# Loading a chunk's edge attributes in five pieces, each begun when the gathers of the preceding piece have landed

## The chip, the cores and the metric

The kernel runs on one core of a Trainium2 chip. The metric is the device time of one execution in microseconds (us), lower is better; of the kernel before it is the median of two runs without the profiler.

## What is computed

A graph has 12,500 nodes with 64 features and 400,000 edges, sorted by destination node. Each edge carries the features of its source node, multiplied by one 64 x 64 matrix, plus its own 64 attributes, multiplied by another, all times a weight. The edges' messages are summed at their destination nodes, added to the nodes, and each node is normalized.

```python
h = feat_src @ node_w.T
rf = review_feat @ review_w.T
m = (h[src_idx] + rf) * edge_w
agg = jax.ops.segment_sum(m, dst_idx, num_segments=12500)
x = _layernorm(x + agg, axis=-1)
```

## The kernel before

Since the matrices can be applied after the sum, the kernel sums 128 raw values per edge (64 features of the source node, 64 attributes) into `sums` at the destination nodes, and multiplies at the end. It does so for two kinds of edges in two ways.

**Gathered edges.** The first 88 chunks of 3200 edges. A chunk lies in one of four slots (`SLOTS`) of `rows`, as 25 tiles of 128 edges (`TILES`, one edge per partition and tile), 64 gathered features and 64 attributes side by side. POOL (`gather_chunk`, L366) fetches the features with one indirect DMA per tile, 25 per chunk. The 25 tiles form five parts of five (`PARTS`, `PER_PART`), and `gathered[s][q]` counts the landings of part q in slot s. Before the first gather of a chunk POOL waits until the chunk's list of source nodes has landed (`src_landed`) and the slot is free (`slot_free`). SP (`load_chunk`) waits for `slot_free` and then loads the chunk's `src`, `dst`, weights and attributes (L310, L313 to L315), the attributes in one DMA of 800 KB. DVE (`add_chunk`) makes a 128 x 128 matrix per tile that says which edge goes to which of 128 nodes, with its weight (`scatter`, L441, three buffers of one part each). PE (`sum_chunk`, L839) multiplies 25 of those by the tiles of `rows` into `window_ps`; it waits for `gathered` and `scatter_ready` before each part. DVE adds the window to `sums` (L453) and then sets `slot_free`.

**Counted edges.** The other 118,400 edges, in 52 groups of 18 tiles (the first has 7). PE and DVE count for each how often a source node occurs (L881, with DVE's L495 and L497; ACT copies each count out, L744), and PE multiplies the counts by the table of nodes held on the chip (`sum_x`, L896, twice 49 pairs per group). ACT loads a group's attributes (`g_attr`, L716, 576 KB) after it has read the counts of the group before.

**Order.** Each engine's program is written out by hand. A step of PE is: sum a chunk, count the 18 tiles of a group, sum a second chunk in three steps of five, then `sum_x`. Eight chunks and five groups make a round (`STEPS` = 2, 1, 2, 1, 2). POOL does nothing but gathers until the last chunk and scales eight blocks of the output afterwards. SP's queue is in order: the four slots are filled first, then 84 chunks as slots come free, then the stores of the output (L351), which wait for ACT and POOL to scale the blocks. After chunk 85 DVE and PE finish all blocks of nodes that chunks 86 and 87 don't reach (`early`), then sum those two chunks and finish the `late` blocks.

Of the kernel before, what the change touches and what calls it, by code (L numbers as in the profile page):

```python
# [36 lines left out]
TILES = 25  # L37
SLOTS = 4
PARTS = 5
# [13 lines left out]
def build(nc, x, src, dst, attr, weight, node_w, review_w, out):  # L53
    NODES, F = x.shape
    EDGES = src.shape[0]
    CHUNK = P * TILES
# [6 lines left out]
    PER_PART = TILES // PARTS  # L63
# [34 lines left out]
    with ExitStack() as ctx:  # L98
        def sb(name, shape, dt=F32):
            return ctx.enter_context(nc.sbuf_tensor(name, shape, dt))  # L100
# [4 lines left out]
        def sem(name):  # L105
            return ctx.enter_context(nc.semaphore(name))
# [4 lines left out]
        rows = sb("rows", [P, SLOTS, TILES, 2 * F])  # L111
# [99 lines left out]
        w_t_ready = sem("w_t_ready")  # L211
        src_landed = [sem(f"src_landed{s}") for s in range(SLOTS)]
        edge_landed = [sem(f"edge_landed{s}") for s in range(SLOTS)]
        gathers_begun = sem("gathers_begun")
        gathered = [[sem(f"gathered{s}_{q}") for q in range(PARTS)] for s in range(SLOTS)]
        slot_free = [sem(f"slot_free{s}") for s in range(SLOTS)]
# [40 lines left out]
        def by_partition(dram, c):  # L257

            return dram[bass.ds(c * CHUNK, CHUNK)].rearrange("(p k) -> p k", k=TILES)
# [36 lines left out]
        def each_chunk(eng, first, until, do):  # L296

            rounds = range(-(-first // SLOTS), until // SLOTS)
            for c in range(first, rounds[0] * SLOTS):
                do(*at_slot(c))  # L300
            with eng.Fori(rounds[0], rounds[-1] + 1) as r:
                for s in range(SLOTS):
                    do(r * SLOTS + s, s, r)
            for c in range((rounds[-1] + 1) * SLOTS, until):
                do(*at_slot(c))

        @block.sync
        def _(sp):
            def load_src(c, s):
                sp.dma_start(src_sb[s][:, :], by_partition(src, c)).then_inc(src_landed[s], 16)  # L310

            def load_rest(c, s):
                sp.dma_start(dst_sb[s][:, :], by_partition(dst, c)).then_inc(edge_landed[s], 16)  # L313
                sp.dma_start(w_sb[s][:, :], by_partition(weights, c)).then_inc(edge_landed[s], 16)
                sp.dma_start(rows[:, s, :, F:2 * F],  # L315
                             attr[bass.ds(c * CHUNK, CHUNK), :].rearrange("(p k) f -> p k f", k=TILES)
                             ).then_inc(edge_landed[s], 16)

            def load_chunk(c, s, r):

                sp.wait_ge(slot_free[s], r + 1)
                load_src(c, s)
                load_rest(c, s)

            for s in range(SLOTS):
                load_src(s, s)
            sp.dma_start(dst_i[:, 0, :], dst.rearrange("(c e) -> c e", e=CHUNK)).then_inc(dst_loaded, 16)

            sp.dma_start(g_dst[1:GROUPS, :, :], dst[COUNTED_FROM + GT0 * P:EDGES].rearrange(
                "(g t e) -> g t e", t=GT, e=P)).then_inc(g_dst_loaded, 16)  # L330
            for t0 in range(0, GT, GT0):
                n = min(GT0, GT - t0)
                sp.dma_start(g_dst[0:1, t0:t0 + n, :], dst[COUNTED_FROM:COUNTED_FROM + n * P].rearrange(
                    "(a t e) -> a t e", a=1, e=P)).then_inc(g_dst_loaded, 16)
            sp.dma_start(w_both[:, 0:F], node_w).then_inc(w_loaded, 16)
            sp.dma_start(w_both[:, F:2 * F], review_w).then_inc(w_loaded, 16)
            for s in range(SLOTS):
                load_rest(s, s)
            each_chunk(sp, SLOTS, CHUNKS, load_chunk)

            sp.wait_ge(tables_ready, 1)
            with sp.If(is_narrow(sp) == 0):
                each_chunk(sp, CHUNKS, ALL_CHUNKS, load_chunk)
            for n, b in enumerate(early + late):
                h0, j = blocks[b]
                if n < ACT_BLOCKS:
                    sp.wait_ge(act_scaled, n + 1)
                else:
                    sp.wait_ge(pool_scaled, n - ACT_BLOCKS + 1)
                whole = min(j, BY_P - h0)  # L350
                sp.dma_start(out[h0 * P:(h0 + whole) * P, :].rearrange("(h l) f -> l h f", l=P),  # L351
                             x_tab[:, h0:h0 + whole, :]).then_inc(stored, 16)
                if whole < j:
                    sp.dma_start(out[BY_P * P:NODES, :], x_tab[0:NODES - BY_P * P, BY_P, :]).then_inc(stored, 16)
            sp.wait_ge(stored, 16 * (BLOCKS + (BY_P < HI)))
# [53 lines left out]
        def _(dve):  # L409
# [9 lines left out]
            def add_chunk(c, s, r, first=None):  # L419


                base = dve.value_load(base_tab[0:1, bass.ds(c, 1)], min_val=0, max_val=NODES - 1)  # L422
                if first is None:
                    first = dve.value_load(window_tab[0:1, bass.ds(c, 1)], min_val=0, max_val=ALL_WINDOWS)
                until = dve.value_load(window_tab[0:1, bass.ds(c + 1, 1)], min_val=0, max_val=ALL_WINDOWS)  # L425

                dve.wait_ge(edge_landed[s], (r + 1) * 48)

                dve.wait_ge(left_ready, first + c + 1)
                dve.tensor_scalar(dst_left[:, :], dst_sb[s][:, :], lo_all[:, bass.ds(c, 1)], None, ALU.subtract  # L430
                                  ).then_inc(left_ready, 1)
                with dve.Fori(first, until) as w:

                    dve.wait_ge(left_ready, w + c + 2)
                    for q in range(PARTS):

                        if q >= PART_BUFS:
                            dve.wait_ge(part_used[q - PART_BUFS], w + 1)
                        for i in range(PER_PART):
                            k = q * PER_PART + i  # L440
                            made = dve.tensor_scalar(scatter[:, q % PART_BUFS, i, :], column[:, :],  # L441
                                                     dst_left[:, k:k + 1], w_sb[s][:, k:k + 1],
                                                     ALU.is_equal, ALU.mult)
                        made.then_inc(scatter_ready[q], 1)

                    dve.wait_ge(window_summed, w + 1)
                    dve.wait_ge(window_added, w + 1)
                    dve.tensor_scalar(dst_left[:, :], dst_left[:, :], float(WIN), None, ALU.subtract  # L448
                                      ).then_inc(left_ready, 1)
                    to = nc.s_assert_within(  # L450
                        base + (w - first) * WIN, 0, NODES - 1, skip_runtime_bounds_check_because=
                        "a chunk's last window begins at or before its largest dst, which is a node")
                    dve.tensor_tensor(sums[:, bass.ds(to, WIN)], sums[:, bass.ds(to, WIN)],  # L453
                                      window_ps[:, 0:WIN], ALU.add).then_inc(window_added, 1)

                dve.sem_inc(slot_free[s], 1)
                return until
# [364 lines left out]
        def _(pe):  # L822
            def sum_chunk(c, s, r, first=None):

                if first is None:
                    first = pe.value_load(window_tab[0:1, bass.ds(c, 1)], min_val=0, max_val=ALL_WINDOWS)
                until = pe.value_load(window_tab[0:1, bass.ds(c + 1, 1)], min_val=0, max_val=ALL_WINDOWS)
                with pe.Fori(first, until) as w:

                    pe.wait_ge(edge_landed[s], (r + 1) * 48)  # L830

                    pe.wait_ge(window_added, w + 1)
                    for k in range(TILES):
                        if k % PER_PART == 0:
                            pe.wait_ge(scatter_ready[k // PER_PART], w + 1)

                            pe.wait_ge(gathered[s][k // PER_PART], (r + 1) * (16 * PER_PART))
                        q, i = divmod(k, PER_PART)
                        done = pe.matmul(window_ps[:, 0:WIN], rows[:, s, k, :], scatter[:, q % PART_BUFS, i, :],  # L839
                                         start=(k == 0), stop=(k == TILES - 1))  # L840
                        if i == PER_PART - 1 and q < PARTS - PART_BUFS:
                            done.then_inc(part_used[q], 1)
                    done.then_inc(window_summed, 1)
                return until
# [157 lines left out]
```

## Time and profile before

| | us |
|---|---|
| median of 2 runs without the profiler | 2815.59 (2814.23 to 2816.95) |
| span of the profiled execution | 4978.1 |
| PE busy in it | 2706.6 |
| POOL busy in it | 2097.5 |
| DVE busy in it | 1848.4 |
| ACT busy in it | 832.4 |

The profiled execution took much longer than those that are timed, so shares of its span are not shares of the time. Durations of single instructions, gaps between instructions that wait for nothing, and the times from an issue to what it releases are what is to be read from it. SPq and ACTq are the queues of SP and ACT, whose DMA issues are not counted as busy; PEclk is the granted TensorE clock as a share of full speed.

### The profile page before, as it was taken

How to read it: one execution, taken by the hardware profiler on the slowest of the kernel's cores; microseconds unless marked ns; L12 is line 12 of the kernel's file. 1: busy time of each engine (PE TensorE's matmuls, PEld its weight loads, DVE VectorE, ACT ScalarE, POOL GpSimd, SP SyncE). 2: the span in 40 equal slices, each digit the busy share in tenths (PEclk: the TensorE clock that was granted, in tenths of full speed). 3: DMA queues.
4: the chain of work that ended last, by engine and by line, in shares of the span. 5: the costliest groups of instructions: out<-in, count | busy, mean ns of one | idle time of the engine just before them, and what ended most of it. 6: DMA issues, size and time to landing. Idle time of an engine off the chain costs nothing.

```text
span 4978.1 us, 63532 instructions
## 1 busy us (share of the span) xinstructions
PE 2706.6 (54%) x22003; PEld 2036.4 (41%) x22004; DVE 1848.4 (37%) x7016; ACT 832.4 (17%) x1327; POOL 2097.5 (42%) x2223
## 2 busy tenths in 40 slices
PE   0555555545655545555456555555554556455465
PEld 0343444434443434444344434344443444344345
DVE  3333333423442333333334424333333344333344
ACT  0111111111121111121111211111111112111112
POOL 7343343443334443444433344434444333544432
PEclk9776777767776767777667767677776777667677
DMA  4111121111111111211111211112111112112111
GB/s 98 37 34 37 34 42 38 34 36 38 37 38 38 34 35 38 41 38 34 35 38 35 42 37 35 34 38 42 38 34 35 37 36 42 37 34 43 36 35 38
DMA packets 531458, 192.11 MB, mean 39 GB/s; under 512 B 489893, under 2 KB 495772, under 8 KB 530975
## 3 DMA queue, kind: packets, MB, share of 16 engines
q1 hardware_dynamic: 334128, 80.80, 8.6%
q0 software_dynamic: 70400, 72.23, 6.6%
q10 hardware_dynamic: 126623, 34.94, 3.2%
q8 instruction: 198, 3.24, 0.3%
q14 instruction: 109, 0.89, 0.1%
HBM read 184.60 MB, written 3.20 MB: 38 GB/s over the span
## 4 chain that ended last, share of the span: by engine, by line
PE 43%; another core or an unknown queue 28%; issue 21%; DVE 4%; ACT 2%; DVEq 1%; ACTq 1%; POOLq 0%; POOL 0%
PE x_sums_ps L896 15%; PE count_ps L881 15%; PE window_ps L839 11%; ACT counts L744 2%; DVE scatter L441 1%; DVE hot_lo L497 1%; PE attr_ps L873 1%; ACTq L771 0%; PE turn_ps L858 0%; PE turn_ps L855 0%; DVEq L422 0%; DVEq L425 0%; DVE hot_key L495 0%; PE count_ps L924 0%
## 5 line engine op out<-in xcount | busy, mean ns | idle before, releaser
L366 POOL DMA_INDIRECT rows<-x,src x2200 | 2088.8, 949 | 2791.5 <-DMA src<-src 2146.3
L881 PE MATMUL count_ps<-hot_key,hot_lo 128*128 128x343 bf16 x5550 | 1157.4, 361 | 1294.2 <-ACT counts L744 839.0
L896 PE MATMUL x_sums_ps<-counts,x_tab 128*64 128x126 f32 (+1 forms) x10192 | 865.5, 302 | 790.2 <-issue 775.0
L881 PEld LDWEIGHTS count_ps<-hot_key,hot_lo 128*128 128x128 bf16 x5550 | 570.1, 113 | 1726.5 <-issue 1092.5
L896 PEld LDWEIGHTS x_sums_ps<-counts,x_tab 128*64 128x64 f32 x10192 | 692.5, 154 | 948.4 <-issue 927.3
L744 ACT ACTIVATE counts<-count_ps 128x686 f32<-128x686 f32 x925 | 737.3, 802 | 1784.9 <-remote 1335.6
L495 DVE TENSOR_SCALAR hot_key<-count,cols 128x686 bf16<-128x686 f16 x925 | 377.8, 408 | 1550.8 <-remote 1272.3
L441 DVE TENSOR_SCALAR scatter<-column,dst_left,w 128x128 f32<-128x128 f32 x2200 | 588.3, 347 | 576.2 <-PE window_ps L839 503.0
L497 DVE TENSOR_SCALAR hot_lo<-count,cols 128x128 bf16<-128x128 f16 x2775 | 721.7, 323 | 4.9 <-issue 4.9
L839 PE MATMUL window_ps<-scatter,rows 128*128 128x128 f32 x4400 | 563.1, 289 | 85.2 <-issue 55.4
L839 PEld LDWEIGHTS window_ps<-scatter,rows 128*128 128x128 f32 x4400 | 535.0, 200 | 120.9 <-issue 108.8
L510 DVE TENSOR_TENSOR hot_rel<-column,cols 128x126 f32<-128x126 f32 (+1 forms) x52 | 15.2, 292 | 645.1 <-issue 441.8
L873 PEld LDWEIGHTS attr_ps<-hot_rel,g_attr 128*128 128x128 f32 x926 | 189.0, 228 | 45.1 <-issue 9.5
L726 ACT ACTIVATE slot_rel<-turn_ps,slot_no 126x1 f32<-126x1 f32 (+1 forms) x52 | 13.6, 262 | 979.2 <-remote 625.3
L873 PE MATMUL attr_ps<-hot_rel,g_attr 128*128 128x14 f32 x926 | 155.2, 243 | 12.6 <-remote 12.6
L759 ACT ACTIVATE x_sums<-x_sums_ps 128x126 f32<-128x126 f32 (+1 forms) x52 | 14.3, 276 | 881.9 <-PE x_sums_ps L896 881.9
L734 ACT ACTIVATE slot_rows<-x_sums_ps 126x128 f32<-126x128 f32 x52 | 14.4, 278 | 400.8 <-PE x_sums_ps L905 400.8
L448 DVE TENSOR_SCALAR dst_left<-dst_left 128x25 f32<-128x25 f32 x88 | 15.8, 180 | 146.8 <-PE window_ps L839 146.8
L531 DVE TENSOR_TENSOR sums<-sums,turn_ps 128x128 f32 x52 | 15.0, 289 | 76.2 <-PE turn_ps L911 43.0
L430 DVE TENSOR_SCALAR dst_left<-dst,lo_all 128x25 f32<-128x25 int32 x88 | 22.3, 254 | 50.2 <-issue 50.2
L405 POOL TENSOR_TENSOR x_tab<-x_tab,counts 128x512 f32<-128x512 f32 (+2 forms) x8 | 5.9, 748 | 79.7 <-DVE counts L573 79.6
L855 PE MATMUL turn_ps<-tile_first,spread 18*126 18x1 f32 (+1 forms) x104 | 19.4, 253 | 33.7 <-DVE packed L484 33.7
(112 smaller groups left out, 557.5 us busy)
## 6 DMA issues: line engine op xcount, KB each, us to landing
rows<-edge_attr SPq DMA_DIRECT2D x88, 800.0 KB
rows<-x,src POOLq DMA_INDIRECT x2200
g_attr<-edge_attr ACTq DMA_DIRECT2D x51, 576.0 KB
out<-x_tab SPq DMA_DIRECT2D x11, 256.0 KB
counts<-dst SPq DMA_DIRECT2D x1, 1562.5 KB
src<-src SPq DMA_DIRECT2D x88, 12.5 KB, 1.7
dst<-dst SPq DMA_DIRECT2D x88, 12.5 KB
w<-edge_weight SPq DMA_DIRECT2D x88, 12.5 KB
```

The costliest lines, as they stand in the source:

```text
L366: pool.indirect_dma_start(out=rows[:, s, k, 0:F], out_offset=None, in_=x, in_offset=bass.IndirectOffsetOnAxis(ap=src_sb[s][:, k:k + 1].bit ...
L430: dve.tensor_scalar(dst_left[:, :], dst_sb[s][:, :], lo_all[:, bass.ds(c, 1)], None, ALU.subtract).then_inc(left_ready, 1)
L441: made = dve.tensor_scalar(scatter[:, q % PART_BUFS, i, :], column[:, :], dst_left[:, k:k + 1], w_sb[s][:, k:k + 1], ALU.is_equal, ALU.mult)
L448: dve.tensor_scalar(dst_left[:, :], dst_left[:, :], float(WIN), None, ALU.subtract).then_inc(left_ready, 1)
L495: dve.tensor_scalar(hot_key[h][:, :], count16[:, :], cols[:, KEY, t:t + 1], None, ALU.is_equal)
L497: made = dve.tensor_scalar(hot_lo[h][:, i, :], count16[:, 0:P], cols[:, LO, t:t + 1], cols[:, part, t:t + 1], ALU.is_equal, ALU.mult)
L744: act.activation(counts[:, :, t * SPAN:(t + 1) * SPAN].rearrange("p (a h) d -> p a h d", a=2), count_ps[t % 2][:, :, 0:HALF].rearrange("p ...
L839: done = pe.matmul(window_ps[:, 0:WIN], rows[:, s, k, :], scatter[:, q % PART_BUFS, i, :], start=(k == 0), stop=(k == TILES - 1))
L855: pe.matmul(turn_ps[0:nt * SPAN, REL_COL:REL_COL + 1], spread[0:nt, 0:nt * SPAN], tile_first[0:nt, 0:1], start=True, stop=True)
L873: pe.matmul(attr_ps[0:(until - t) * F, t * SPAN:until * SPAN], g_attr[:, t:until, :].rearrange("p t f -> p (t f)"), hot_rel[:, t:until, :] ...
L881: last = pe.matmul(count_ps[b][:, a, 0:HALF], hot_lo[h][:, i, :], hot_key[h][:, a * HALF:(a + 1) * HALF], start=(i == 0), stop=(i == 2))
L896: done = pe.matmul(x_sums_ps[half * F:(half + 1) * F, 0:ns], x_tab[:, hi, :], counts[:, hi, 0:ns], start=(hi < 2), stop=(hi >= HI - 2))
```

## The change

The one DMA that loads a chunk's attributes becomes five, one for each part of five tiles (128 x 5 x 64 values, 160 KB). They have semaphores of their own, `attr_landed`, one per slot. For the first four chunks the five are issued in a row. For each of the 84 chunks after them SP issues the first at once, and before piece q waits until part q-1 of the gathers of the same chunk has landed. DVE's wait for `dst` and the weights falls from 48 to 32, since two DMAs are left on `edge_landed`, and PE waits before a window for these and for all five pieces.

```diff
--- before.py
+++ after.py
@@ -211,6 +211,7 @@
         w_t_ready = sem("w_t_ready")
         src_landed = [sem(f"src_landed{s}") for s in range(SLOTS)]
         edge_landed = [sem(f"edge_landed{s}") for s in range(SLOTS)]
+        attr_landed = [sem(f"attr_landed{s}") for s in range(SLOTS)]
         gathers_begun = sem("gathers_begun")
         gathered = [[sem(f"gathered{s}_{q}") for q in range(PARTS)] for s in range(SLOTS)]
         slot_free = [sem(f"slot_free{s}") for s in range(SLOTS)]
@@ -309,18 +310,30 @@
             def load_src(c, s):
                 sp.dma_start(src_sb[s][:, :], by_partition(src, c)).then_inc(src_landed[s], 16)
 
-            def load_rest(c, s):
+            def load_edges(c, s):
                 sp.dma_start(dst_sb[s][:, :], by_partition(dst, c)).then_inc(edge_landed[s], 16)
                 sp.dma_start(w_sb[s][:, :], by_partition(weights, c)).then_inc(edge_landed[s], 16)
-                sp.dma_start(rows[:, s, :, F:2 * F],
-                             attr[bass.ds(c * CHUNK, CHUNK), :].rearrange("(p k) f -> p k f", k=TILES)
-                             ).then_inc(edge_landed[s], 16)
+
+            def load_attr_part(c, s, q):
+                ks = slice(q * PER_PART, (q + 1) * PER_PART)
+                sp.dma_start(rows[:, s, ks, F:2 * F],
+                             attr[bass.ds(c * CHUNK, CHUNK), :].rearrange("(p k) f -> p k f", k=TILES)[:, ks, :]
+                             ).then_inc(attr_landed[s], 16)
+
+            def load_rest(c, s):
+                load_edges(c, s)
+                for q in range(PARTS):
+                    load_attr_part(c, s, q)
 
             def load_chunk(c, s, r):
 
                 sp.wait_ge(slot_free[s], r + 1)
                 load_src(c, s)
-                load_rest(c, s)
+                load_edges(c, s)
+                load_attr_part(c, s, 0)
+                for q in range(1, PARTS):
+                    sp.wait_ge(gathered[s][q - 1], (r + 1) * (16 * PER_PART))
+                    load_attr_part(c, s, q)
 
             for s in range(SLOTS):
                 load_src(s, s)
@@ -424,7 +437,7 @@
                     first = dve.value_load(window_tab[0:1, bass.ds(c, 1)], min_val=0, max_val=ALL_WINDOWS)
                 until = dve.value_load(window_tab[0:1, bass.ds(c + 1, 1)], min_val=0, max_val=ALL_WINDOWS)
 
-                dve.wait_ge(edge_landed[s], (r + 1) * 48)
+                dve.wait_ge(edge_landed[s], (r + 1) * 32)
 
                 dve.wait_ge(left_ready, first + c + 1)
                 dve.tensor_scalar(dst_left[:, :], dst_sb[s][:, :], lo_all[:, bass.ds(c, 1)], None, ALU.subtract
@@ -827,7 +840,8 @@
                 until = pe.value_load(window_tab[0:1, bass.ds(c + 1, 1)], min_val=0, max_val=ALL_WINDOWS)
                 with pe.Fori(first, until) as w:
 
-                    pe.wait_ge(edge_landed[s], (r + 1) * 48)
+                    pe.wait_ge(edge_landed[s], (r + 1) * 32)
+                    pe.wait_ge(attr_landed[s], (r + 1) * (16 * PARTS))
 
                     pe.wait_ge(window_added, w + 1)
                     for k in range(TILES):
```

SP's queue, in the loop over the rounds of four slots. What stood there for slots 1 and 2 (a row "ISA" is a wait or an address):

```order
L310 ISA [waits slot_free1]
L310 DMA src<-src 128x25
L313 DMA dst<-dst 128x25
L314 DMA w<-edge_weight 128x25
L315 ISA
L315 DMA rows<-edge_attr 128x25x64
L310 ISA [waits slot_free2]
L310 DMA src<-src 128x25
```

And what stands there now, from the first attribute piece of slot 1 to the first load of slot 2 (the three small loads of slot 1 stand ahead of it as before):

```order
L319 DMA rows<-edge_attr 128x5x64
L319 ISA [waits gathered1_0]
L319 DMA rows<-edge_attr 128x5x64
L319 ISA [waits gathered1_1]
L319 DMA rows<-edge_attr 128x5x64
L319 ISA [waits gathered1_2]
L319 DMA rows<-edge_attr 128x5x64
L319 ISA [waits gathered1_3]
L319 DMA rows<-edge_attr 128x5x64
L311 ISA [waits slot_free2]
L311 DMA src<-src 128x25
```

The loads of slot 2 now stand behind four waits for the gathers of slot 1.

PE's queue, at the first window of a chunk in slot 0. Before:

```order
L832 REGISTER_ALU [waits edge_landed0]
L837 REGISTER_ALU [waits scatter_ready0,window_added]
L839 MATMUL window_ps<-scatter,rows 128x128 [waits gathered0_0]
L839 MATMUL window_ps<-scatter,rows 128x128 x4
L839 MATMUL window_ps<-scatter,rows 128x128 [waits gathered0_1,scatter_ready1]
```

Now:

```order
L844 REGISTER_ALU [waits edge_landed0]
L846 REGISTER_ALU [waits attr_landed0]
L853 MATMUL window_ps<-scatter,rows 128x128 [waits gathered0_0,scatter_ready0,window_added]
L853 MATMUL window_ps<-scatter,rows 128x128 x4
L853 MATMUL window_ps<-scatter,rows 128x128 [waits gathered0_1,scatter_ready1]
```

The wait for all five pieces stands ahead of the first matmul of the window; the waits for single parts of the gathers are where they were.

## Rows read from the trace of the kernel before

**Rows 1.** the page: span, and busy time of each engine (share of the span), x instructions.

```profile
span 4978.1 us, 63532 instructions
...
PE 2706.6 (54%) x22003; PEld 2036.4 (41%) x22004; DVE 1848.4 (37%) x7016; ACT 832.4 (17%) x1327; POOL 2097.5 (42%) x2223
```

**Rows 2.** the waits: engine, line, waited for: us in total, times, longest.

```profile
POOL rows L366 <- DMA src<-src: 2146.3, 84, 40.2
ACT counts L744 <- remote: 1335.6, 186, 20.2
...
POOL rows L366 <- issue: 645.2, 2116, 0.7
```

**Rows 3.** the waits of SP's queue, same columns.

```profile
SPq L310 <- DVEq L456: 4596.1, 84, 104.8
```

**Rows 4.** groups by line: count, busy us, mean ns, idle before and its releaser.

```profile
L366 POOL DMA_INDIRECT rows<-x,src x2200 | 2088.8, 949 | 2791.5 <-DMA src<-src 2146.3
```

**Rows 5.** timeline of POOL: start us, us, engine, line, operation, count, idle before.

```profile
4.43 1.12 POOL L366 DMA_INDIRECT rows<-x,src  x1 [0.66 <-issue]
...
34.56 0.95 POOL L366 DMA_INDIRECT rows<-x,src  x1 [0.30 <-issue]
35.81 0.94 POOL L366 DMA_INDIRECT rows<-x,src  x1 [0.30 <-issue]
...
4883.11 0.94 POOL L366 DMA_INDIRECT rows<-x,src  x1 [0.30 <-issue]
```

**Rows 6.** timeline of PE, same columns; then windows with the granted clock (PEclk).

```profile
2048.46 6.32 PE L839 MATMUL window_ps<-scatter,rows 128*128 128x128 f32 x50 [0.53 <-DVE scatter L441]
...
2054.94 5.59 PE L896 MATMUL x_sums_ps<-counts,x_tab 128*64 128x126 f32 x98
...
2150.51 2.02 PE L881 MATMUL count_ps<-hot_key,hot_lo 128*128 128x343 bf16 x12
...
core 0: us, PE busy (x) PEld busy (x) DVE busy (x) ACT busy (x) POOL busy (x), PEclk, DMA share, GB/s
2048.50:2054.70 6.20, 6.20 (x51) 5.94 (x52) 4.85 (x19) 0.58 (x3) 0.00 (x0) 1.00 0.46 98
2055.00:2060.40 5.40, 5.40 (x99) 5.29 (x98) 2.76 (x13) 0.00 (x0) 1.96 (x2) 1.00 0.49 100
```

**Rows 7.** timeline of all engines around two chunk loads, same columns.

```profile
2001.71 0.29 DVE L453 TENSOR_TENSOR sums<-sums,window_ps 128x128 f32 x1
...
2002.11 0.34 SPq L310 DMA_DIRECT2D src<-src  x1
...
2003.59 0.56 SPq L315 DMA_DIRECT2D rows<-edge_attr  x1
...
2004.64 0.94 POOL L366 DMA_INDIRECT rows<-x,src  x1 [25.95 <-DMA src<-src]
...
2034.75 0.94 POOL L366 DMA_INDIRECT rows<-x,src  x1 [0.31 <-issue]
...
2055.49 0.34 SPq L310 DMA_DIRECT2D src<-src  x1
...
2058.02 1.02 POOL L366 DMA_INDIRECT rows<-x,src  x1 [22.33 <-DMA src<-src]
```

**Rows 8.** DMA in 2035.6 to 2036.3, 2036.3 to 2036.9, 2036.9 to 2048.9: packets, MB, rate or share.

```profile
DMA packets 0, 0.00 MB, mean 0 GB/s; under 512 B 0, under 2 KB 0, under 8 KB 0
...
q0 software_dynamic: 32, 0.03, 28.3%
...
DMA packets 1, 0.02 MB, mean 1 GB/s; under 512 B 0, under 2 KB 0, under 8 KB 0
```

**Rows 9.** DMA queues in 2004.6 to 2008.2 (three rows), then in 2004.9 to 2009.5.

```profile
DMA packets 2949, 0.76 MB, mean 212 GB/s; under 512 B 2948, under 2 KB 2948, under 8 KB 2948
...
q1 hardware_dynamic: 2948, 0.75, 104.6%
q14 instruction: 1, 0.01, 1.2%
...
q1 hardware_dynamic: 3216, 0.82, 90.6%
q0 software_dynamic: 89, 0.09, 8.8%
```

**Rows 10.** the ACT issue of g_attr, and the DMA queues in 2048.9 to 2052.4.

```profile
2048.13 0.40 ACTq L716 DMA_DIRECT2D g_attr<-edge_attr  x1
...
q10 hardware_dynamic: 2320, 0.59, 80.8%
```

**Rows 11.** timeline of the end, all engines.

```profile
4942.41 17.16 SPq L351 DMA_DIRECT2D out<-x_tab  x13
...
4955.03 7.18 PE L839 MATMUL window_ps<-scatter,rows 128*128 128x128 f32 x50 [3.68 <-issue]
4959.61 1.07 SPq L354 DMA_DIRECT2D out<-x_tab  x1
```

## Prediction

> **What bounds the kernel now.** I first read the span on the page: the profiled execution took 4978.1 us [rows 1], against a median of 2815.6 us for the runs without the profiler. So the profile is 1.77 times as long as what is to be predicted, and the first question is where its extra 2162 us lie. The list of waits answers: POOL, which issues the 2200 gathers, idled 2146.3 us in 84 pieces before the first gather of a chunk, waiting for its `src` load [rows 2]. That load is not slow. SP's own waits show why it is late: SP sat 4596.1 us, also 84 times, for DVE's `slot_free` [rows 3]. The slots came free late, because in the profiled execution PE, DVE and ACT stood still for long stretches: the copy of the counts alone waited 1335.6 us for something that the profile doesn't name, up to 20 us at a time [rows 2].
>
> The groups by line then give POOL's own pace: a gather is busy for 949 ns [rows 4] and 645.2 us of issue gaps lie over 2116 of them [rows 2], 0.305 us each. One gather takes 1.254 us, a chunk of 25 takes 31.4 us, and all take 2088.8 + 645.2 = 2734 us. They start at 4.4 us [rows 5]. 2815.6 - 4.4 - 2734 leaves 77 us for everything behind the last gather and for all stalls; in the profile the time behind the start of the last gather at 4883.1 is 95 us [rows 5]. So without the profiler POOL hardly waits, and it is the bound. The chunk boundary at 35.81 us, where everything was loaded ahead, shows that a chunk then begins with the ordinary gap of 0.30 us [rows 5].
>
> PE is second. Where the granted clock is 1.00, the upper of its two levels, a window of 25 tiles takes 6.3 us, half a sum over x 5.6 us and two counted tiles 2.0 us [rows 6]. A step with its 18 tiles and 1.6 chunks is about 18.2 + 11.2 + 10.1 = 39.5 us, against 1.6 x 31.4 = 50 us of POOL. So PE catches up with the gathers and then waits for them, while POOL stays three chunks (94 us) ahead of the slot that it needs next. Before the change SP has that lead too: it loads a chunk as soon as its slot is free.
>
> **The change, part by part.** *Same bytes.* 800 KB per chunk and 3200 pieces of 256 bytes go as before; four more issues and four waits per chunk cost nothing on SP, which idles [rows 3]. DVE needs only the two small loads (its wait falls from 48 to 32) and was never short of the third: 0. At the start (four slots filled with no wait) nothing but the number of issues changes.
>
> *SP loses its lead.* This is what matters. SP now stands in the middle of chunk n, waiting for its gathers, and behind that wait are queued the loads of chunk n+1, `src` first. POOL cannot begin n+1 without them. So each of the 84 chunks after the first four gets a chain that must fit into the time of its last five gathers. From the start of chunk n, in us:
> - tile 19, the last of the fourth part, starts at 19 x 1.254 = 23.8;
> - it lands at most 2.15 later, at 26.0: a gather issued at 2034.75 [rows 7] had no packet before 2036.3, its 32 packets until 2036.9 and none after [rows 8];
> - SP wakes 0.1 later, as it does when DVE frees a slot (2001.71 + 0.29 to 2002.11) [rows 7]: 26.1;
> - it issues the fifth piece, at most the 0.56 of the whole load [rows 7] and a gap of 0.1: 26.8;
> - from the issue of `src` to the first gather is 2.53 us, at 2002.11 to 2004.64 and at 2055.49 to 2058.02 [rows 7]: 29.3;
> - the `src` packets queue behind those of the piece in the same ring. The burst of the whole load, 3216 packets, took 4.6 us [rows 9], so 640 packets take 0.9. The delay is 0 to 0.9; I take all: 30.2.
>
> POOL needs it at 31.4. The slack is 1.2 us (2.1 with no queueing), so the undisturbed chain is hidden and POOL's pace stays.
>
> *Disturbed chains.* ACT loads 576 KB of `g_attr` for each group, a burst of 2320 packets from 2048.9 to at most 2052.4 after an issue at 2048.13 [rows 10]. What a burst does to a gather is seen at 2004.64: it had no packet of its own until 2008.2 [rows 9], 3.6 us after its issue where 1.55 is usual [rows 8], so 2.0 us late. When does the `g_attr` burst fall? PE ends a window some 3.8 us into the next chunk's gathers (below), counts 18 tiles in 18.2, and ACT issues at 22.0; packets run from 22.8 to 26.3. The gather of tile 19 has its packets at 25.4 to 26.0, inside that. This holds for the three steps of five whose first chunk finds PE waiting, 31 of the 51 loads. In the other two PE comes some 5 us later out of a sum over x, and the burst meets the `src` load or nothing. A chain late by 2.0 stalls POOL for 2.0 - 1.2 = 0.8 us, or for nothing with the slack of 2.1. I take the middle, 0.4 us, x 31 = 12 us. Bounds: 0, and 0.8 x 51 = 41 us.
>
> *PE waits for all five pieces.* It used to start a window when the first gathers were there; now it starts when the fifth piece has landed, at 26.1 + 1.4 + 0.9 = 28.4 (the whole load had its first packets 1.3 to 1.4 us after its issue [rows 7, 9]). A window is 6.3 to 7.2 us [rows 6, 11], so it ends at 34.7 to 35.6. Before, it ended a fifth of a window behind the last landing, 30.1 + 2.15 + 1.3 = 33.6. For all chunks but the last these 1 to 2 us are covered by POOL's lead of 94 us; the last one sets the end: +2 us.
>
> *The stores.* SP cannot store the early blocks until it has issued the fifth piece of chunk 87. The thirteen stores took 17.2 us of issue in the profile and ended at 4959.6, before the last window did at 4962.2 [rows 11]. They start here some 10 us later than before and still end before the late blocks are ready: 0, at most 5 us.
>
> **Sum.** 0 + 12 + 2 = 14 us. The terms are durations of gathers, packets and issues, which I take over unscaled to the unprofiled 2815.6: 2830 us. For the profiled execution itself the sum is different: its slots come free 50 us apart and more (SP's `src` issues at 2002.11 and 2055.49 [rows 7]), longer than the 29 us for which SP is tied up, so the chain costs nothing there and the span should be 4978 + 2 = 4980, within 1%. The profile will hide the stall that I expect without the profiler.
>
> **Rivals.**
> 1. *The bursts cost nothing*: the slack is nearer 2.1, or the `g_attr` loads fall elsewhere, or PE is the bound without the profiler after all (2706.6 us busy at a mixed clock [rows 1]), so that slots come free late as in the profile. For it: the queueing term was taken at its bound. Against it: the 3.6 us of that one gather. Time: 2815.6 + 2 = 2818. The Trainium skill says the same by another way: "DMA: Bandwidth & Descriptors", section "Queues, rings and completion order", has each DMA engine round-robin between queues and change after some 9 to 17 descriptors, so a gather would never wait for a whole burst. By the packet pace of this trace, 4.6 us for 200 packets on an engine [rows 9], 17 of them are 0.4 us, less than the slack, which gives 2818. The gather at 2004.64 speaks against that rule, since no packet of it moved for 3.6 us.
> 2. *Slower: the chain is too long in every chunk.* Place: POOL before the first gather of each of 84 chunks, waiting for `src`. It decides (2%, 56 us, is 0.67 us per chunk) from a chain 1.9 us longer than my sum. For it: six terms in a row, none ever seen in this combination; a gather delayed by 2.0 in each chunk would give 0.8 x 84 = 67 us, and `src` delayed by another 2.0 gives 2.8 x 84 = 235 us. Against it: four of the six terms stand in rows, and the rest is taken at its bound. Time, midway: 2815.6 + 150 = 2966.
> 3. *A little faster*: the burst of 3200 packets at a chunk's load no longer disturbs the gathers. Gathers average 949 ns where the undisturbed ones are 0.94 us [rows 4, 5]: at most some 9 ns x 2200 = 20 us, of which half may belong to DVE or `g_attr`. Time: 2806. Landings of gathers are not on POOL's path, so nothing more can come.
>
> **How the numbers follow.** The forecast of 2830: 0.38. Nothing but the tail, 2818: 0.30. Too long in every chunk, 2966: 0.17. A little faster: 0.07. The remaining 0.08 are stalls of 45 to 80 us from more collisions than counted. Within 2% is 2759 to 2872, about what a measurement of this kernel can tell from no change. It takes in the forecast, rivals 1 and 3 and most of the rest: 0.80. Slower is 0.18, faster 0.02, since no term exceeds 20 us of gain. The range of 2806 to 2885 leaves out most of rival 2 and little else.
>
> **What would show it.** In the profile after: five attr issues per chunk, four of them 6.3 us apart; SP waiting for gathers; POOL's first gather of a chunk never more than 2.6 us behind its `src` issue; POOL's total wait for `src` near 2146. POOL's gathers should stay at 949 ns. If the median is above 2872, the chain is longer than 33 us and the term at fault is the landing or the `src` load behind the piece. If it is 2818 or less, bursts don't delay gathers enough. If the span of the profile grows by over 1%, then SP's order bites even where slots come free 50 us apart.

## The result and the profile after

The changed kernel takes 2850.09 us (2843.94 and 2856.24), the kernel before 2815.59: 1.0126 times as long, 95% interval 1.0071 to 1.0181 (two runs of each), so 20 to 51 us slower. The forecast was 2830 in a range of 2806 to 2885.

One thing must be said ahead of all rows. These kernels have two paces, far apart: the kernel before takes 2812 to 2817 us on some chips and 4916 to 5006 on others. The two times above are of the first kind, and so is the profile of the changed kernel. The profile of before (4978.1 us, [rows 1]) was of the second. I call them quick and slow chips.

Page of the changed kernel, on a quick chip: span, busy times, the chain that ended last, POOL's group (count, busy us, mean ns, idle before).

```profile
span 2854.4 us, 64593 instructions
...
PE 2231.2 (78%) x22003; PEld 1851.0 (65%) x22004; DVE 1813.1 (64%) x7016; ACT 838.0 (29%) x1327; POOL 2128.2 (75%) x2223
...
POOL 67%; issue 24%; DMA 7%; SPq 1%; PE 0%; DVE 0%; POOLq 0%; ACT 0%; DVEq 0%
...
L379 POOL DMA_INDIRECT rows<-x,src x2200 | 2119.6, 963 | 704.9 <-issue 661.7
```

Its waits (engine, line, waited for: us in total, times, longest), and then those of SP's queue.

```profile
POOL rows L379 <- issue: 661.7, 2170, 0.7
...
PE window_ps L853 <- DMA rows<-edge_attr: 499.7, 51, 24.1
...
POOL rows L379 <- DMA src<-src: 43.2, 30, 3.0
```

```profile
SPq L319 <- DMA rows<-x,src: 2361.8, 334, 56.2
SPq L311 <- DVEq L469: 20.5, 1, 20.5
```

Beside [rows 2 to 4]: POOL's wait for `src` is 43.2 us in 30 pieces instead of 2146.3 in 84. SP no longer waits for a free slot (one time, at the start) but for gathers, 334 of the 336 times. POOL is the bound: 2119.6 + 661.7 + 43.2 = 2824.5 us from the first gather at 4.4, and 26 us of finish. Without waits the same sum has 30 more ordinary gaps of 0.305 in place of the 43.2: the pure stall is 43.2 - 9.2 = 34.0 us, where 34.5 (20 to 51) were lost. One of the 30 is no longer than an ordinary gap, so there are 29 stalls. PE's 499.7 us of waiting for the pieces hold nobody up before the last chunk, since no slot is waited for after the start.

**One stall.** The chain that ended last shows what the stalls are made of (start, us, what), in two places.

```profile
1344.97 4.72 DMA rows<-x,src
...
1350.41 2.14 DMA src<-src
...
1409.11 4.12 DMA rows<-x,src
1414.37 2.02 DMA src<-src
```

The gather that begins at 1344.97 is tile 19 of its chunk. It lands 4.72 us later. The one that begins at 1377.15, in the next chunk, is tile 19 with nothing in its way. The timelines of ACT, SP and POOL around both (start, us, engine, line; POOL's idle time before in brackets):

```profile
1344.93 0.40 ACTq L729 DMA_DIRECT2D g_attr<-edge_attr  x1
...
1350.41 0.37 SPq L311 DMA_DIRECT2D src<-src  x1
...
1353.38 0.94 POOL L379 DMA_INDIRECT rows<-x,src  x1 [1.20 <-DMA src<-src]
...
1377.15 0.95 POOL L379 DMA_INDIRECT rows<-x,src  x1 [0.31 <-issue]
...
1380.26 0.39 SPq L311 DMA_DIRECT2D src<-src  x1
...
1384.64 0.95 POOL L379 DMA_INDIRECT rows<-x,src  x1 [0.30 <-issue]
```

In the free chunk `src` is issued 3.11 us after tile 19 began. In the other ACT issued `g_attr` in the same moment as tile 19; `src` was issued after 5.44 us, 2.33 later, and the first gather of the next chunk came 8.41 us after tile 19 instead of 7.49. From the issue of `src` to that gather are 2.97 us. So the free chain is 3.11 + 2.97 = 6.08 us, the slack 1.41, and 2.33 - 1.41 = 0.92 is the stall (1.20 less the ordinary 0.30).

**Longer stalls.** Here the burst comes later, at the `src` load itself:

```profile
316.40 0.40 ACTq L729 DMA_DIRECT2D g_attr<-edge_attr  x1
...
317.33 0.38 SPq L311 DMA_DIRECT2D src<-src  x1
...
323.79 0.95 POOL L379 DMA_INDIRECT rows<-x,src  x1 [2.37 <-DMA src<-src]
```

`src` was issued in time, and the gather came 6.46 us after it instead of 2.97: 3.49 us late, the length of a whole `g_attr` burst (3.5 us at most, [rows 10]).

The longest wait of all is again one of tile 19, which begins at 1922.44 (the chain, then the timeline):

```profile
1922.44 6.03 DMA rows<-x,src
```

```profile
1922.12 0.40 ACTq L729 DMA_DIRECT2D g_attr<-edge_attr  x1
...
1929.62 0.34 SPq L311 DMA_DIRECT2D src<-src  x1
...
1932.67 0.94 POOL L379 DMA_INDIRECT rows<-x,src  x1 [3.04 <-DMA src<-src]
```

Of the 16 parts in which this gather's landing is counted, 15 were there after 4.45 us, as in the first stall, and the last after 6.03. A last part more than 1 us behind the others is found in the three longest waits (3.04, 2.97 and 2.60 us) and in no other. In each of the three, one 16 KB packet of the instruction queue began 3.2 to 3.8 us after tile 19 and took 1.2 to 1.3 us; such packets stand beside several shorter stalls too, and no run tests whether it is what held up the last part.

**All stalls.** ACT's issues of `g_attr` from the fifth chunk on, by their distance from the start of tile 19 of the chunk in which they fall:

| issued | loads | followed by a stall |
|---|---|---|
| 19.1 to 6.3 us before tile 19 | 3 | 0 |
| 0.4 before to 2.3 after | 29 | 29 |
| 3.6 to 6.6 after | 17 | 0 |

No chunk without such a load has a stall. In 22 of the 29 the landing of tile 19 is late, so that `src` is issued 4.4 to 7.3 us after it (3.1 to 3.9 in chunks with no load of `g_attr`). In the other 7 `src` goes out in time and its own load is late. This ties the loss of POOL to the bursts in the complete kernel, at the quick pace, by the trace alone.

### The profile page after: what moved, and what is told of

The parts are those of the page before. It is cut to its first block, busy times and chain, and to the rows that moved or that the text cites. A ratio compares the mean times of both kernels' runs of the same rounds, so it can differ in the third digit from the quotient of the medians.

```text
span 2854.4 us, 64593 instructions
## 1 busy us (share of the span) xinstructions
PE 2231.2 (78%) x22003; PEld 1851.0 (65%) x22004; DVE 1813.1 (64%) x7016; ACT 838.0 (29%) x1327; POOL 2128.2 (75%) x2223
## 4 chain that ended last, share of the span: by engine, by line
POOL 67%; issue 24%; DMA 7%; SPq 1%; PE 0%; DVE 0%; POOLq 0%; ACT 0%; DVEq 0%
POOL rows L379 67%; DMA rows<-x,src 4%; DMA src<-src 3%; SPq L319 0%; PE window_ps L853 0%; DVE scatter L454 0%; SPq L311 0%; DMA rows<-edge_attr 0%; POOLq L302 0%; POOLq L377 0%; SPq L302 0%; POOL count L387 0%; DVE x_tab L562 0%; DVE counts L581 0%; POOLq L98 0%
## 5 line engine op out<-in xcount | busy, mean ns | idle before, releaser
L379 POOL DMA_INDIRECT rows<-x,src x2200 | 2119.6, 963 | 704.9 <-issue 661.7
L853 PE MATMUL window_ps<-scatter,rows 128*128 128x128 f32 x4400 | 631.1, 310 | 543.7 <-DMA rows<-edge_attr 499.7
L853 PEld LDWEIGHTS window_ps<-scatter,rows 128*128 128x128 f32 x4400 | 604.7, 222 | 577.9 <-issue 560.9
L895 PE MATMUL count_ps<-hot_key,hot_lo 128*128 128x343 bf16 x5550 | 933.5, 310 | 0.0
L895 PEld LDWEIGHTS count_ps<-hot_key,hot_lo 128*128 128x128 bf16 x5550 | 507.8, 102 | 304.9 <-issue 116.4
L910 PE MATMUL x_sums_ps<-counts,x_tab 128*64 128x126 f32 (+1 forms) x10192 | 576.1, 271 | 13.1 <-ACT counts L757 13.0
L910 PEld LDWEIGHTS x_sums_ps<-counts,x_tab 128*64 128x64 f32 x10192 | 551.7, 137 | 22.4 <-ACT counts L757 15.4
L887 PEld LDWEIGHTS attr_ps<-hot_rel,g_attr 128*128 128x128 f32 x926 | 154.5, 190 | 27.3 <-issue 7.3
L887 PE MATMUL attr_ps<-hot_rel,g_attr 128*128 128x14 f32 x926 | 136.5, 222 | 7.0 <-DVE hot_lo L510 7.0
L466 DVE TENSOR_TENSOR sums<-sums,window_ps 128x128 f32 x88 | 25.4, 288 | 5.3
## 6 DMA issues: line engine op xcount, KB each, us to landing
src<-src SPq DMA_DIRECT2D x88, 12.5 KB
dst<-dst SPq DMA_DIRECT2D x88, 12.5 KB
w<-edge_weight SPq DMA_DIRECT2D x88, 12.5 KB
```

The costliest lines, as they stand in the source:

```text
L379: pool.indirect_dma_start(out=rows[:, s, k, 0:F], out_offset=None, in_=x, in_offset=bass.IndirectOffsetOnAxis(ap=src_sb[s][:, k:k + 1].bit ...
L887: pe.matmul(attr_ps[0:(until - t) * F, t * SPAN:until * SPAN], g_attr[:, t:until, :].rearrange("p t f -> p (t f)"), hot_rel[:, t:until, :] ...
L895: last = pe.matmul(count_ps[b][:, a, 0:HALF], hot_lo[h][:, i, :], hot_key[h][:, a * HALF:(a + 1) * HALF], start=(i == 0), stop=(i == 2))
L910: done = pe.matmul(x_sums_ps[half * F:(half + 1) * F, 0:ns], x_tab[:, hi, :], counts[:, hi, 0:ns], start=(hi < 2), stop=(hi >= HI - 2))
```

## The experiments

Three theories. **A**: the loss is POOL waiting for `src`, which SP now issues behind its waits for gathers, in chunks where a `g_attr` burst uses up the slack. **B**: the pieces themselves, more DMAs and later ones beside the gathers, slow POOL or the landings. **C**: the chain is too long in every chunk.

### First four, on a slow chip

The changed kernel again:

> The changed kernel once more, on the chip of the next three runs, to measure its loss beside them. Both theories: 1.0126 times the kernel before, within 0.5%. In its profile POOL's first gather of about 30 of the 83 later chunks waits for src, 35 us over the ordinary gaps in all.

Then with `src`, `dst` and weights one chunk ahead:

```diff
     load_attr_part(c, s, 0)
+    load_next_small(c, s, r)      # waits slot_free of the next slot; src, dst, weights of c + 1
     for q in range(1, PARTS):
         sp.wait_ge(gathered[s][q - 1], (r + 1) * (16 * PER_PART))
         load_attr_part(c, s, q)
```

> The changed kernel, but SP issues src, dst and weights of chunk n+1 behind the first attribute piece of chunk n, ahead of the four waits for gathers. Theory A (the loss is POOL waiting for a src load that is queued behind those waits): POOL's stalls for src vanish, 35 us come back, and what is left is the later start of PE's last window: 2815 + 5 = 2820 us, ratio to the kernel before 1.002. Theory B (the pieces themselves, more DMAs beside the gathers, slow POOL or the landings): the time stays at 2850, ratio 1.012.

Without the waits:

```diff
     for q in range(1, PARTS):
-        sp.wait_ge(gathered[s][q - 1], (r + 1) * (16 * PER_PART))
         load_attr_part(c, s, q)
```

> The changed kernel without the waits for gathers: five pieces, issued in a row as soon as the slot is free; PE still waits for all five. Theory A: SP keeps its lead, so no stall for src, and the pieces of the last chunk have landed long before PE needs them: 2815 us, ratio 1.000. Theory B (five DMAs instead of one cost time by their number): 2830 to 2850. The span of its profile is open: near 2820 if the pieces by themselves free the profiled execution of its standstills, near 4980 if their spacing does it.

And with the last wait one part later:

```diff
-        sp.wait_ge(gathered[s][q - 1], (r + 1) * (16 * PER_PART))
+        sp.wait_ge(gathered[s][q if q == PARTS - 1 else q - 1], (r + 1) * (16 * PER_PART))
```

> The changed kernel, but the fifth piece waits for the landing of the fifth part of the gathers instead of the fourth, so that SP is tied up for five gathers (6.3 us) longer. Theory A with the sum of the chain as the profile of the changed kernel shows it (2.6 + 0.6 + 3.0 = 6.2 us from tile 19 to the first gather, against 7.5 available): 1.3 us of slack become a stall of 5.0 us at each of 84 chunks, 2817 + 84 x 5.0 = 3240 us, and some 50 us more from g_attr bursts that no slack absorbs: 3240 to 3300, ratio 1.15 to 1.17. Theory B: 2855, since the number of DMAs is the same.

| kernel | us | ratio to before (4987.15 us), 95% |
|---|---|---|
| changed | 5001.08 | 1.0027 (1.0014 to 1.0039) |
| src ahead | 5015.66 | 1.0057 (1.0037 to 1.0077) |
| no waits | 5019.89 | 1.0066 (1.0046 to 1.0086) |
| last wait a part later | 5014.55 | 1.0056 (1.0037 to 1.0075) |

Hardly any of the expectations could be tested here, since they were written for the other pace; the 1.0126 expected of the changed kernel was missed with 1.0027. Even the kernel whose chain is 6.3 us longer in each chunk, which should have cost over 400 us, lies with the rest. The waits of the changed kernel on this chip say why; POOL's first, then SP's:

```profile
POOL rows L379 <- DMA src<-src: 2176.0, 84, 41.1
ACT counts L757 <- remote: 1236.5, 159, 20.9
```

```profile
SPq L311 <- DVEq L469: 2280.3, 84, 102.6
SPq L319 <- DMA rows<-x,src: 423.5, 73, 8.6
```

They are those of [rows 2, 3]: slots come free late, SP is mostly done with a chunk's pieces before the next slot is free, and its order hardly matters. That is what the prediction said of the profiled execution (it forecast a span within 1% of 4978; it is 5005.5, +0.5%). What it shows for the question is little: all four take 0.3 to 0.7% longer than the kernel before at this pace, the three variants more than the changed kernel and not told apart from each other, and no run separates the number of DMAs from PE's wait for all five. One part of the third expectation falls: the pieces do not end the standstills, with or without their spacing (spans 5005.5 and 5015.7).

The kernel with `src` ahead ran twice more, on two further occasions:

> The changed kernel with src, dst and weights of the next chunk issued ahead of the four waits for gathers, once more, since the first time the kernel before itself took 4987 us. If the kernel before takes about 2815 us here: theory A (the loss is POOL waiting for src behind SP's waits): ratio 1.002, and its profile shows no boundary gap over 0.4 us between chunks; theory B (the pieces slow POOL or the landings): ratio 1.012. If the kernel before takes about 4980 us, both: 1.003 to 1.007, as in the first time, since slots come free too late for SP's order to matter.

> The changed kernel with src, dst and weights of the next chunk issued ahead of the four waits for gathers, on another chip. If the kernel before takes about 2815 us here: theory A (the loss is POOL waiting for src behind SP's waits): ratio 1.002, no gap over 0.4 us between chunks on POOL; theory B (the pieces slow POOL): ratio 1.012. If the kernel before takes about 4985 us: 1.003 to 1.007 as twice already.

Both were slow chips again: 5021.43 against 4994.02 (1.0055, 1.0041 to 1.0069) and 4972.64 against 4920.08 (1.0098, 1.0080 to 1.0116), the second above the 1.007 expected. So this repair of the complete kernel has never been timed at the quick pace.

### A cut-down in which POOL is the bound on any chip

PE does one matmul per window, DVE one scatter matrix, and the counted edges are left out; SP and POOL do for the 88 chunks what they did. In the version with bursts ACT loads 576 KB into `g_attr` for each chunk. The edit, shortened (`...`):

```diff
+    dve.tensor_scalar(scatter[:, 0, 0, :], ...)           # one tile instead of 25
+    pe.matmul(window_ps[:, 0:WIN], rows[:, s, TILES - 1, :], scatter[:, 0, 0, :], start=True, stop=True)
+    # bursts, on ACT, for each chunk from the fifth on:
+    act.wait_ge(gathered[s][3], (r + 1) * (16 * PER_PART))
+    act.dma_start(g_attr[:, :, :], ...)
```

> A cut-down of the kernel before, meant to make POOL the bound whatever the chip: the counted edges are left out on all engines, PE does one matmul per chunk and DVE one scatter matrix, so the output is not the reference's. SP's and POOL's programs are those of the kernel before. If the other engines no longer hold POOL up: 84 x 25 gathers and more at 1.254 us, last gather begun at 4.4 + 2199 x 1.254 = 2762 us, no boundary gap between chunks over 0.4 us, and some 50 us of finish: 2815 us. If it still takes over 4000 us, the standstills do not come from the work of PE, DVE and ACT, and nothing below can be read.

> The same cut-down with SP's program of the changed kernel: five pieces, four waits for gathers, no g_attr loads at all. Theory A (a chain of 6.2 us from tile 19 to the next chunk's first gather, in 7.5 us): every chain fits, boundary gaps stay at 0.3 us, and the time is that of the cut-down before within 5 us. Theory C (the chain alone is too long in every chunk, my rival for slower): gaps above 0.3 at all 84 boundaries, 67 us or more in all. Theory B (the pieces slow the gathers): the mean gather above that of the cut-down before by 10 ns or more.

> The cut-down with the changed order, and ACT loads 576 KB into g_attr each time that the fourth part of a chunk's gathers has landed, just when SP issues the fifth piece and src. Theory A (a g_attr burst delays what meets it by up to its own 3.4 us, and 1.3 us of it are slack): 2.1 us of gap at each of 84 boundaries, 176 us more than the cut-down with the changed order (bounds 60 to 250). Theory B (bursts are harmless, queues take turns): under 10 us more.

> The cut-down with the changed order, but the fifth piece waits for the fifth part of the gathers instead of the fourth: the chain begins five gathers (6.27 us) later. Theory A: slack of 1.3 us becomes a stall of 5.0 us, 84 x 5.0 = 420 us more than the cut-down with the changed order, POOL's gaps at the boundaries 5.3 us each. If slack and chain were not as summed, the gap is off by as much: 6.3 us each (529 us in all) with no slack, under 3 us with a slack over 3.

These four ran on one slow chip (the kernel before took 4983.99 there); POOL's group in each, in the order of the table:

```profile
L364 POOL DMA_INDIRECT rows<-x,src x2200 | 2339.6, 1063 | 725.6 <-issue 725.6
```

```profile
L377 POOL DMA_INDIRECT rows<-x,src x2200 | 2296.1, 1044 | 759.3 <-issue 759.3
```

```profile
L378 POOL DMA_INDIRECT rows<-x,src x2200 | 2243.6, 1020 | 812.2 <-issue 803.6
```

```profile
L377 POOL DMA_INDIRECT rows<-x,src x2200 | 2075.8, 944 | 1092.8 <-issue 763.9
```

| cut-down | us | gathers busy | gaps |
|---|---|---|---|
| order of before | 3145.64 | 2339.6 | 725.6 |
| changed order | 3134.92 | 2296.1 | 759.3 |
| changed order, bursts | 3135.41 | 2243.6 | 812.2 |
| changed order, last wait a part later | 3233.00 | 2075.8 | 1092.8 |

The last one is the sharp test of the chain, and it came out as summed. The ordinary gaps of 2200 gathers are 671 us; 1092.8 - 671 = 422 us of stall, 5.02 for each of 84 chunks, where 5.0 and 420 were expected. (The first of the 84 has none, because SP waits for no gathers ahead of its loads; the median of the other 83 is 4.9.) One boundary of it:

```profile
1506.73 0.94 POOL L377 DMA_INDIRECT rows<-x,src  x1 [0.30 <-issue]
1509.35 0.37 SPq L319 DMA_DIRECT2D rows<-edge_attr  x1
1509.92 0.37 SPq L311 DMA_DIRECT2D src<-src  x1
...
1512.90 0.94 POOL L377 DMA_INDIRECT rows<-x,src  x1 [5.23 <-DMA src<-src]
```

Tile 24 begins at 1506.73; the piece is issued 2.62 later, `src` 0.57 after it, and the next gather 2.98 after that: 6.17 us, against the 6.2 of the expectation.

The other three did not go as expected. The first is 330 us over its 2815, and the bursts cost 0.5 us instead of 176. The gaps did grow, by 53 us from the second to the third, but the gathers became shorter by as much (52.5). In these three, busy time and gaps add to 3055 to 3065 us whatever the split: without a pause a gather takes 1.39 us all told on this chip, not 1.25, as if stalls of a microsecond or so were paid from that. What sets that pace I have not found. For theory A against B this part is inconclusive, except that the pieces did not make gathers longer (1063 to 1044).

### The two that decide, on a quick chip

> The cut-down whose fifth piece waits for the fifth part (3233 us, 5.4 us of gap at each boundary), with src, dst and weights of the next chunk issued ahead of the waits. The same waits, the same pieces; only src no longer stands behind them. Theory A (the gaps are POOL waiting for src): gaps back to 0.3 us at every boundary, 422 us of gaps gone; the time falls to that of the cut-downs without gaps, 3125 to 3150 us, because gathers without a pause run at 1.37 to 1.40 us each there and not at 1.25. Theory B (the waits or the late pieces hold POOL up in another way, by slot_free or by PE's late window): gaps stay near 5 us and the time near 3233.

> The cut-down with a g_attr load at the landing of each fourth part (1.5 us of gap at each of 84 boundaries, 102 us in all), with src, dst and weights issued ahead of the waits. Theory A (a burst costs POOL time only through the late src): gaps back to 0.3 us. Theory B (a burst holds the gathers up by itself): gaps stay above 0.5 us or the mean gather grows by 20 ns or more over the 1020 ns of the run with gaps, more than the pause that is gone explains. The time, by the pace of gathers without pauses seen so far: 3125 to 3150 us.

This time the kernel before took 2814.06 us. With `src` ahead of the waits, the kernel with the latest fifth piece took 2811.53 (ratio to before 0.9992, 0.9981 to 1.0004), the one with a burst in every chunk 2808.89 (0.9980, 0.9969 to 0.9991). POOL's group and SP's wait for gathers, first of the former, then of the latter:

```profile
L395 POOL DMA_INDIRECT rows<-x,src x2200 | 2075.8, 944 | 670.8 <-issue 670.8
```

```profile
SPq L319 <- DMA rows<-x,src: 2321.3, 336, 65.3
```

```profile
L396 POOL DMA_INDIRECT rows<-x,src x2200 | 2076.2, 944 | 670.8 <-issue 670.8
```

```profile
SPq L320 <- DMA rows<-x,src: 2298.9, 336, 65.1
```

SP waits 336 times, nearly as long in all as in the changed kernel (2361.8 us), the pieces come as late or later, each chunk has its burst, and POOL has no gap beyond the ordinary 670.8 us; a gather takes 944 ns. Against the cut-down with the same waits but `src` behind them, 422 us of stall are gone at equal gathers (944 both). That other one ran on a slow chip, and neither has a twin at its own pace; but a gap of 0.3 us at every boundary leaves nothing for B to explain. So B is ruled out for the waits, for the pieces and for these bursts: in the cut-down none of them costs POOL anything but through `src`. The bursts fall behind tile 19 here; for those that delay tile 19 itself the evidence is the table of all stalls above. The expected times (3125 and more) missed, since they took over the pace of the slow chip.

## Why the prediction was right, point by point

**POOL is the bound without the profiler**: right, 67% of the chain that ended last. The reading behind it, that the 2162 us of difference were stalls of PE, DVE and ACT, was right in the main (POOL's wait is 2146.3 of them), but the profiler did not cause them: a slow chip has them without it.

**The chain of 6.4 us** (23.8 to 30.2): measured 6.08 in a free chunk, and 6.17 in the cut-down. Its terms: tile 19 to the piece 2.62 (summed 2.3), piece to `src` 0.57 (0.7), `src` to the gather 2.97 (2.53 + at most 0.9 = 3.4). The slack of 1.2 to 2.1 was 1.4. So C fell: 55 of 84 chunks have no stall. One sign did not come: POOL's first gather was to be at most 2.6 us behind its `src` issue, and it was 2.97 in a stall and up to 6.46, and up to 3.8 on a slow chip.

**Collisions**: the kind of place was right and the count too, 29 stalls where 31 were forecast. The size was not: "I take the middle, 0.4 us, x 31 = 12 us"; it is 34.0 / 29 = 1.17 us. The step that failed is that middle, taken between a stall of 0.8 and none. The delay of 2.0 was nearly right. In 19 of the stalls tile 19 is late in the ordinary way, `src` is issued 5.4 us after it (the median) instead of 3.1, 2.3 late, and a slack of 1.4 leaves 0.9 us; these 19 add up to 17.8 us. Two things were not in the sum. The three long stalls, with one part of the gather later still, add 7.7 us. And the seven in which the burst hits the `src` load, 1.8 to 3.5 us late, add 8.8: in the prediction that case stood for the other steps of PE, without a price.

There was luck in the count. ACT was to issue `g_attr` 22.0 us into a chunk; in the 29 it did so at 23.9 to 26.4. By the prediction's own times, a burst until 26.3 and packets of tile 19 due at 25.4, the gather would have been 0.9 late at most, less than any slack. The stalls came because the bursts came later than summed.

**Rival 1**, that bursts are free, is refuted here: the gather at 1344.97 landed 4.72 us after its issue, where the median on the page of the changed kernel is 2.5. "DMA: Bandwidth & Descriptors" in the Trainium skill, "Queues, rings and completion order", has the engines take turns at packets, of some 9 to 17 descriptors typically and of 64 at most. This trace does not agree with 17, which would be 0.4 us. A turn of 64 would be 1.5 us by the same pace, an estimate; the first packet of the gather at 2004.64 came 2.0 us late [rows 8, 9], and how many turns it waited for, no run shows.

```profile
rows<-x,src POOLq DMA_INDIRECT x2200, 2.5
```

**The tail**: forecast +2 us. The end of the changed kernel (from the chain that ended last):

```profile
2821.07 2.41 DMA rows<-x,src
2823.63 2.45 DMA rows<-edge_attr
...
2826.42 2.49 PE window_ps L853 x10
...
2834.05 4.14 PE window_ps L853 x20
```

The fifth piece of the last chunk landed 2.45 us after its issue (summed: 2.3), and only then did PE begin, at 2826.42. The last gather began at 2827.3 and landed by about 2829.8, after which the old kernel has a fifth of a window to do. PE ended at 2838.2. My estimate is a loss of 4 to 7 us instead of 2: inside the window PE also waited for DVE, which could make its last ten scatter matrices only then and took 6.35 us for them, while POOL scaled the output, where the fifteen before had taken 3.97. This was not tried: no run took PE's wait for all five pieces apart. With 34 us of stalls and this the sum is 38 to 41, inside the interval of 20 to 51. The stores cost nothing, as forecast: SP had issued thirteen by 2839.9, before the late blocks were scaled (2844.9).

**Gathers stay at 949 ns**: no, 963. But this is not the change: in the cut-downs without work on DVE the quick chip has 944, so about 20 ns x 2200 = 43 us of the time are what POOL loses beside the other engines, before and after alike as far as can be told (the kernel before has no profile of that pace). The 77 us that the prediction left "for everything behind the last gather and for all stalls" were no sign of stalls either: its 2734 us leave out the 84 ordinary gaps at the chunk boundaries (26 us, since [rows 2] counts 645.2 without them), gathers of 963 instead of 949 ns are 31, and some 20 are left for the finish.

**The profile of the changed kernel** was forecast at 4980 us. It came from a quick chip and shows what that forecast said the profile would hide. On a slow chip the forecast held (5005.5 us, POOL's wait 2176.0 near 2146).

## What to carry to other kernels

In an in-order queue a wait delays what stands behind it, so look there first: the pieces did POOL no harm, the 12.5 KB list behind them did. Where a load must be issued late, issue the small loads of the next round ahead of it. A slack of 1.4 us is none where another queue sends bursts of 3.5 us; what met one was 1.3 to 4.1 us late here, so a forecast needs the full delay at each meeting and not half of it. Before a profile is trusted, its span has to be held against the times.

## What the hardware showed unexpectedly

The same program takes 2814 or 4987 us. One slow chip was met twice, slow both times (4987 and 4920); whether the pace belongs to the chip or to the occasion is not told apart by so few. In the slow pace PE, DVE and ACT do little from some microseconds into 25 gathers in a row until after the last. In the profile of before, beside the gathers of [rows 7] that began at 2058.02, PE's matmuls of the sum over x, which have nothing to wait for, came singly (start, us, and the idle time before in brackets):

```profile
2080.14 0.37 PE L896 MATMUL x_sums_ps<-counts,x_tab 128*64 128x126 f32 x1 [2.45 <-issue]
2082.94 0.37 PE L896 MATMUL x_sums_ps<-counts,x_tab 128*64 128x126 f32 x1 [2.43 <-issue]
```

Without gathers 98 of them took 5.59 us [rows 6]. In windows of the same profile (columns as in [rows 6]), before the gathers, at their start and further on:

```profile
2050.00:2058.00 8.00, 8.00 (x98) 7.62 (x98) 5.24 (x24) 0.00 (x0) 0.00 (x0) 1.00 0.30 57
2058.00:2064.00 6.00, 4.78 (x70) 4.09 (x67) 1.04 (x6) 0.00 (x0) 4.76 (x5) 1.00 0.80 163
2074.00:2089.00 15.00, 2.22 (x6) 0.91 (x5) 5.72 (x21) 0.00 (x0) 11.34 (x13) 0.50 0.12 26
```

Left open: what differs between the two paces, and why, in the cut-downs, gathers without a pause take 1.39 us on the slow chip where they take 1.25 with a pause of 5 us after every 25.
